# Keys transposed by DMA, a reordered state-space part, and sums copied by two engines in a decoder layer

## The reference

```python
# mixer(x): xn = rmsnorm(x); two Mamba2 passes, forward on channels 0:64, backward in time on 64:128;
#           each: in-projection, causal convolution of width 4, SiLU, state recurrence over 1024 steps,
#           y = (scan + D * xs) * silu(z), y = rmsnorm(y) * w, out-projection; x + concat @ op_w.T + op_b
x = layernorm(x + mixer(x))
q = layernorm(x) @ Wq + bq;  k, v = split(concat([layernorm(ctx), layernorm(x)]) @ Wkv + bkv)   # 8 heads of 128
x = layernorm(x + softmax(q @ k.T / sqrt(128)) @ v @ Wo + bo)
x = layernorm(x + shared_expert(xn) + top2_of_8_experts(xn))      # xn = layernorm(x)
```

## Time and profile before

| | |
|---|---|
| median of 3 runs | 1732.46 us (1732.25 to 1732.76) |
| profiled execution | 1731.69 us, span of its instructions 1729.7 us |
| PE busy | 1673.7 us (97%) |
| DVE busy | 1306.2 us (76%) |
| ACT busy | 1087.5 us (63%) |
| POOL busy | 882.5 us (51%) |
| mean granted TensorE clock | 0.988 of 2.4 GHz |
| HBM read and written | 15.27 MB, 4.23 MB |

### The profile page before, as it was taken

How to read it: one execution, slowest core, us unless ns; L and a number is a source line. 1 busy time by engine, 2 the same in 40 slices (tenths; PEclk the granted TensorE clock), 3 DMA queues, 4 the chain that set the end, 5 groups by cost and what they waited for, 6 DMA issues and landing times.

```text
span 1729.7 us, 32116 instructions
## 1 busy us (share of the span) xinstructions
PE 1673.7 (97%) x9213; PEld 856.4 (50%) x9213; DVE 1306.2 (76%) x2302; ACT 1087.5 (63%) x1333; POOL 882.5 (51%) x724
## 2 busy tenths in 40 slices
PE   6878999999999999999999999999999999999996
PEld 4855444444444444445444444445454544444585
DVE  7968998877777767777777777776767777777667
ACT  4555666666666666666666666666566666667664
POOL 4845994035454545454555545454545454551365
PEclk9989999999999999999999999999999999999998
DMA  5001110000000000000000000000000000000201
GB/s 183 2 1 37 56 55 5 1 1 1 1 0 1 0 0 0 0 0 0 0 0 1 0 0 1 1 0 1 0 0 0 1 0 0 0 1 1 55 25 44
DMA packets 20611, 20.58 MB, mean 12 GB/s; under 512 B 6655, under 2 KB 18179, under 8 KB 20150
## 3 DMA queue, kind: packets, MB, share of 16 engines
q1 hardware_dynamic: 19414, 17.20, 3.2%
q0 software_dynamic: 1120, 2.31, 0.4%
HBM read 15.27 MB, written 4.23 MB: 11 GB/s over the span
## 4 chain that ended last, share of the span: by engine, by line
PE 88%; DVE 4%; ACT 3%; issue 3%; POOL 1%; DMA 1%; SPq 0%; ACTq 0%; POOLq 0%; DVEq 0%
PE PS L1936 87%; ACT p_arena L1095 1%; POOL xg_dram L849 1%; DVE mxs L1790 1%; ACT p_arena L1088 1%; POOL p_arena L858 0%; PE PS L2265 0%; SPq L651 0%; DVE w_arena L1278 0%; DVE w_arena L1452 0%; DMA a_arena<-xg_dram 0%; DMA w_arena<-in_x 0%; ACT z_arena L925 0%; DVE z_arena L1834 0%; ACT p_arena L1079 0%
## 5 line engine op out<-in xcount | busy, mean ns | idle before, releaser
L803 POOL TENSOR_TENSOR p_arena<-p_arena 128x512 f16<-128x512 f32 x364 | 604.3, 1660 | 668.4 <-ACT p_arena L1088 668.4
L1079 ACT ACTIVATE p_arena<-PS 128x1024 f16<-128x1024 f32 (+1 forms) x480 | 484.8, 1010 | 504.8 <-PE PS L1936 504.6
L1497 DVE TENSOR_REDUCE mxs<-PS 128x512 f32 (+1 forms) x900 | 600.5, 671 | 197.2 <-PE PS L1936 195.2
L1936 PE MATMUL PS<-a_arena,z_arena 128*128 128x512 f16 (+1 forms) x2832 | 747.2, 380 | 1.4 <-DVE a_arena L1805 1.4
L1936 PE MATMUL PS<-p_arena,z_arena 128*128 128x512 f16 x2800 | 740.4, 379 | 1.4 <-ACT p_arena L1095 0.3
L1088 ACT ACTIVATE p_arena<-PS 128x1024 f32<-128x1024 f32 (+1 forms) x480 | 481.6, 1003 | 0.0
L1529 DVE TENSOR_TENSOR p_arena<-p_arena 128x512 f16<-128x512 f32 (+1 forms) x480 | 381.5, 795 | 97.9 <-ACT p_arena L1088 91.8
L1936 PEld LDWEIGHTS PS<-a_arena,z_arena 128*128 (+1 forms) x2832 | 274.6, 98 | 326.5 <-issue 2.2
L1936 PEld LDWEIGHTS PS<-p_arena,z_arena 128*128 128x128 f16 (+1 forms) x2800 | 270.5, 98 | 318.0 <-ACT p_arena L1095 8.8
L1936 PE MATMUL PS<-z_arena,a_arena 128*128 (+3 forms) x1024 | 353.9, 361 | 3.1 <-DVE mxs L1790 1.3
L1936 PEld LDWEIGHTS PS<-z_arena,a_arena 128*128 128x128 f16 (+1 forms) x1024 | 98.3, 98 | 123.2 <-DVE mxs L1790 4.5
(11 more groups left out here) (328 smaller groups left out, 1022.4 us busy)
## 6 DMA issues: line engine op xcount, KB each, us to landing
w_arena<-in_L_ffn_gate_up_w SPq DMA_DIRECT2D x8, 512.0 KB, 3.3
p_arena<-in_ctx SPq DMA_DIRECT2D x2, 1600.0 KB, 9.2
w_arena<-in_L_ffn_down_w SPq DMA_DIRECT2D x8, 256.0 KB, 3.7
a_arena<-in_L_xattn_Wkv SPq DMA_DIRECT2D x1, 1024.0 KB, 5.8
a_arena<-xg_dram SPq DMA_DIRECT2D x12, 65.0 KB, 2.0
xg_dram<-VO SPq DMA_DIRECT2D x1, 715.0 KB, 7.6
xg_dram<-VO SPq DMA_DIRECT2D x1, 650.0 KB, 9.0
w_arena<-in_x SPq DMA_DIRECT2D x1, 512.0 KB, 4.3
```

The lines of the kernel that those rows point to most:

```text
L803: g.tensor_tensor(Plo[:, r % 3, QB:2 * QB], P32[:, r % 2, QB:2 * QB], Phi[:, r % 3, QB:2 * QB], ALU.subtract).then_inc(pl_ready, 1)
L1079: s.activation(Phi[:, r % 3, 0:w], ps, ACT.Exp, scale=1 / SSC).then_inc(hi_ready, 1)
L1497: v.tensor_reduce(mxs[:, i, bass.ds(kb, 1)], PS[:, 6 + par, 0:w], AX.X, ALU.max).then_inc(mx_read, 1)
L1936: return t.matmul(o, l, r, start=start, stop=stop)
```

## The change

1. **Keys by DMA.** The 50 context chunks are no longer transposed by PE and copied by ACT. SP issues DMA transfers with transposition from `Zhi` to `ZThi` (28, 14 and 8 chunks, after the casts they need and after the last gated row, since the target memory was in use by then) and from `Zlo` to `ZTlo` (28 and 22 chunks). Only the four left rows stay with PE and ACT (`turned_left`). PE waits for all high keys before the first product of the maxes, for the low ones after the last.
2. **State-space part.** Convolution 0 goes before the second group of dt products; the three products for the decays come after convolution 2 instead of 3, and eight instead of ten convolutions run ahead of the loop. `rows` is split into `decay_rows` and `turned_rows`, which with `gram(0)` go between convolutions 4 and 7, each waiting only for the SiLUs it needs. Aggregates and root of the context's first half move from before the loop into chunk 0; the other side work moves one chunk later.
3. **Early roots.** The sums of squares of chunks 0 to 5 (`SOON`) are brought together in chunk 6 and their root is taken in chunk 7; ACT loads the root's table in chunk 5. Behind the loop 12 of the 16 additions to x are done first, those of chunks 6 and 7 (`LATER`) after a second root, some statistics between. The last multiplication of each Newton step is joined with the scaling after it. The latents' rows are signalled in two halves, and `a_side(0)` starts after the first.
4. **Bias rows** lie in other memory, are loaded before the context and split by POOL before the diagonal matrices.
5. **Order behind the loop**: casts 5, 6 and 7 between the projections, the left keys after the second, the root of the latents between heads 1 and 2. In the maxes the projections of the later heads start one pair later.
6. **Sums.** At step 1 of a block ACT copies bank 4 and DVE bank 5; PE waits for both.

The diff, cut to its core (lines that are only moved or renamed are left out where they repeat the list above):

```diff
@@ -354,6 +353,8 @@
         take = carve(r_arena)
         R0, R00 = take([2, QB])[0:1], take([2, QB])[0:1]
         take = carve(r_arena)
+        brow = take([H * D])
+        take = carve(r_arena)
         xfT = take([T])
...
         CONV = [(0, 0), (0, 1), (0, 2), (1, 0), (1, 1), (1, 2), (0, 3), (1, 3)]
-        AHEAD = 2
+        BESIDE = 4
+        NSOON = 6
+        SOON, LATER = slice(0, NSOON), slice(NSOON, TC)
         DECAY, TURNED_XB, GRAM, STATE, FROM_STATE, INSIDE, GATE = range(7)
         def conv_bank(n):
-            return (1, 2, 3, 4, 5, 6, 7, 1, 7, 6)[n] if n < 8 + AHEAD else 7
+            return (6, 1, 2, 3, 4, 5, 7, 6)[n] if n < 8 else 7
...
-        N_KEYS = len(KV_GROUPS) + 1
-        KEYS_FIRST = 10
-        BEHIND_LOOP = [("out", 0), ("wide", 0), ("keys", 2), ("keys", 3), ("joint", 0), ("wide", 1), ("cast", 6), ("keys", 4), ("root", 0),
-                       ("keys", 5), ("joint", 1), ("cast", 7), ("wide", 2), ("keys", 6), ("keys", 7), ("left", 0), ("joint", 2),
-                       ("latents", 0), ("keys", 8), ("keys", 9)]
...
+        BEHIND_LOOP = [("out", 0), ("cast", 5), ("wide", 0), ("cast", 6), ("joint", 0), ("cast", 7), ("wide", 1), ("left", 0), ("joint", 1),
+                       ("root", 0), ("wide", 2), ("joint", 2), ("latents", 0)]
+        LATE0 = 2
...
+            def turned_keys(s_parts, first, parts, src, dst, done):
+                sp.wait_ge(s_parts, first + parts.stop)
+                c0, w = CTX0 + HI_PARTS[parts.start][0], sum(HI_PARTS[i][1] for i in parts)
+                sp.dma_start(dst[:, c0 * P:(c0 + w) * P].rearrange("p (c n) -> p c n", n=P), src[:, c0:c0 + w, :],
+                             transpose=True).then_inc(done, 16)
+            sp.wait_ge(yg_done, TC)
+            for parts in HI_TURNS:
+                turned_keys(z_hi, 0, parts, Zhi, ZThi, zt_hi)
             sp.wait_ge(z_lo, 1)
             sp.dma_start(Zhi[32:32 + LEFT, 0, :], Zlo[0:LEFT, 0, :]).then_inc(left_st, 16)
             sp.dma_start(Zhi[64:64 + LEFT, 0, :], Zhi[0:LEFT, 0, :]).then_inc(left_st, 16)
+            for parts in LOW_TURNS:
+                turned_keys(z_lo, 1, parts, Zlo, ZTlo, zt_lo)
             sp.wait_ge(zlT_v, 2)
             sp.wait_ge(z_lo, N_HI + 1)
...
-            pool.wait_ge(ld_mw, N_MW)
-            for q in range(2):
-                last = g.tensor_scalar(diagD[:, q], I32[:], V["D_" + "fb"[q]], None, ALU.mult)
-            last.then_inc(diag_ready, 1)
-            pool.wait_ge(ld_b, 48)
+            pool.wait_ge(ld_nd, N_ND)
             g.tensor_scalar(brow[0:3, :], brow[0:3, :], BS, None, ALU.mult).then_inc(brow_ready, 1)
             pool.wait_ge(brow_ready, 1)
             g.tensor_copy(b16[0:3, :], brow[0:3, :]).then_inc(brow_ready, 1)
             pool.wait_ge(brow_ready, 2)
             g.tensor_tensor(b16[32:35, :], brow[0:3, :], b16[0:3, :], ALU.subtract).then_inc(brow_ready, 1)
             pool.wait_ge(brow_ready, 3)
+            pool.wait_ge(ld_mw, N_MW)
...
-                if c == 0:
-                    for n in range(8, 8 + AHEAD):
-                        silu_conv(n)
-                if c < 3:
-                    silu_conv(8 + AHEAD + 2 * c)
+                if c < BESIDE:
+                    silu_conv(8 + 2 * c)
+                if c == TC - 1:
+                    root(2)
+                if 2 <= c < NSOON - 1:
+                    high_ctx(c - 2)
+                elif c == NSOON - 1:
+                    s.activation(rt[:, 5, 0:1], iota8[:, 0:1], ACT.Sqrt)
+                elif c == NSOON:
+                    high_ctx(c - 3)
                 if c:
-                if c >= 2:
-                    silu_conv(9 + AHEAD + 2 * c)
+                if c < BESIDE:
+                    silu_conv(9 + 2 * c)
                 act.wait_ge(yg_done, c + 1)
                 for q in range(2):
                     if c or q:
                         act.wait_ge(sq_done, 2 * c + q)
...
+            for n in range(6):
                 silu_conv(n)
             state_rows(0)
+            for n in range(6, 8):
+                silu_conv(n)
             for c in range(TC):
...
-            for k in range(2):
-                turned_keys(k, ZThi, zt_hi)
+            high_ctx(4)
+            gate_out(TC - 1)
+            root(3)
...
-                    turned_keys(k, ZThi, zt_hi)
                 elif kind == "root":
-                    root(3)
+                    root(4)
                 elif kind == "left":
                     act.wait_ge(z_scaled, CC + 1)
                     s.copy(Zhi[0:LEFT, 0, :], ctxl[:]).then_inc(z_hi, 1)
+                    turned_left(ZThi, 1, 2)
...
-                s.copy(U_sb, PS[:, 4:6, :]).then_inc(u_evac, 1)
+                s.copy(U_sb[:, 0], PS[:, 4, :]).then_inc(u_evac, 1)
...
                 dve.wait_ge(sq_out, k)
-                settle(v.reciprocal(rs[:, 3, 0:w], rs[:, 1, 0:w]))
+                settle(v.tensor_tensor(at(1), at(3), at(3), ALU.mult))
+                settle(v.tensor_tensor(at(1), at(1), at(0), ALU.mult))
+                settle(v.tensor_scalar(at(1), at(1), -0.5, 1.5, ALU.mult, ALU.add))
...
@@ -1388,6 +1379,8 @@
                 dve.wait_ge(yi_ps, c + 1)
                 dve.wait_ge(t1_done, c + 1)
+                if c == 0:
+                    dve.wait_ge(silu_done, 8)
                 if c >= 2:
                     dve.wait_ge(gt_ps, c - 1)
...
+                if c == TC - 1:
+                    dve.wait_ge(z_scaled, CC // 2)
                     inputs(c + 1)
...
                     settle(v.bn_stats(st6[0:LEFT, CC, :], ctxl[:]))
-                elif c == 2:
+                elif c == 3:
                     ctx_aggr(CC // 2, CC)
                     settle(v.bn_aggr(mv[0:LEFT, CC, :], st6[0:LEFT, CC, :]))
                     for piece in range(5):
                         last = v.tensor_copy(VO[:, h, :, D:D + 1], I32[:, 0:1].unsqueeze(1).to_broadcast([P, 2, 1]))
                     last.then_inc(t_ready, 1)
+                    dve.wait_ge(ss_ps, 1)
+                    dve.wait_ge(sq_done, 2 * NSOON)
+                    chunk_root(2, SOON, PS[:, 7, SOON])
+            def mixed_in(q, part):
+                for c in range(TC)[part]:
+                    t, at = place(q, c), q * TC + c
+                                                  op0=ALU.mult, op1=ALU.add)
+                return last
...
+            dve.wait_ge(out_evac, NSOON)
+            mixed_in(0, SOON)
+            dve.wait_ge(ss_ps, 2)
+            dve.wait_ge(sq_done, 2 * TC)
+            chunk_root(3, LATER, PS[:, 0, 0:TC - NSOON])
+            settle(mixed_in(1, SOON))
+            row_stats(range(TC - NSOON, NSOON))
+            chunk_scale(3, LATER)
             dve.wait_ge(out_evac, TC)
-            dve.wait_ge(z_scaled, CC + 1)
+            mixed_in(0, LATER)
+            settle(mixed_in(1, LATER))
...
-            dve.wait_ge(sq_done, 2 * TC)
-            v.tensor_copy(ssy[:, 1, :], PS[:, 0, 0:TC]).then_inc(yo_used, 1)
-            dve.wait_ge(yo_used, 1)
-            inv_root(2, 2 * TC, ssy[:].rearrange("p q c -> p (q c)"), 1.0 / D)
-            for q in range(2):
-                for c in range(TC):
-                    at = q * TC + c
-                    if c == 0 and q:
-                        settle(last)
-                    last = v.scalar_tensor_tensor(out=x_sb[:, c, :], in0=yo[:, q, c, :], scalar=rs[:, 3, at:at + 1], in1=x_sb[:, c, :],
-                                                  op0=ALU.mult, op1=ALU.add)
...
+                return v.tensor_scalar(dst, src, mv[:, t, 0:1], rs[:, 3, at + t:at + t + 1], ALU.subtract, ALU.mult)
...
+            v.tensor_scalar(rs[:, 0, TC:2 * TC], mv[:, 0:TC, 1], 1.0 + EPS, EPS * EPS, ALU.mult, ALU.add).then_inc(sq_in, 1)
+            for half in range(2):
+                for c in range(HT * half, HT * half + HT):
+                    last = norm_row(zl[:, c, 1:D], x_sb[:, c, 1:D], c, TC)
+                last.then_inc(zl_ready, 1)
...
+                    if st == 1 and not first:
+                        dve.wait_ge(pv_done, NS * j)
+                        v.tensor_copy(U_sb[:, 1], PS[:, 5, :]).then_inc(u_evac, 1)
...
+            pe.wait_ge(w_sb, 2)
+            for n, (q, b) in enumerate(X_ORDER):
+                pe.wait_ge(xT_lo, n + 1)
+                if n == 1:
+                    convolve(0)
...
+            convolve(1)
...
             convolve(2)
-            convolve(3)
...
+                if c < BESIDE:
+                    convolve(9 + 2 * c)
+                if c == NSOON:
+                    pe.wait_ge(sq_done, 2 * NSOON)
+                    mm(PS[:, 7, SOON], J32[:], ssy[:, 1, SOON]).then_inc(ss_ps, 1)
+            convolve(3)
+            convolve(4)
             pe.wait_ge(dt_a, 4)
-            pe.wait_ge(silu_done, 8)
+            decay_rows(0)
+            convolve(5)
+            pe.wait_ge(op_sb, 3)
+            convolve(6)
+            pe.wait_ge(silu_done, 5)
+            turned_rows(0)
+            pe.wait_ge(silu_done, 6)
```

(23 more changed lines are left out.)

232 lines of the change are left out of this document (85 added, 147 removed).

## The result

The changed kernel took 1723.92 us (median of 5 executions, 1721.67 to 1724.7) beside 1732.76 for the kernel before: the ratio is 0.9945, with a 95% interval of 0.993 to 0.9959. It is 8.8 us faster where 14.4 were forecast; the time lies in the forecast range (1709 to 1731), but the likeliest case (1713 to 1722) missed it by 2 us. The profiled execution is the shortest of the five (1721.67, span 1719.7; before 1731.69 and 1729.7), so its rows explain 10.0 us.

The account below looks back on a forecast made before the run. PE bounds the middle blocks, a chain of waits the stretch behind the chunk loop. Gains of 7.3 (to the first product), 3.5 (maxes) and 3.6 (sums) make 14.4: 1731.7 - 14.4 + 0.8 = 1718 us, range 1709 to 1731.

Parts of the forecast that it names:

- likeliest case: Whole kernel: the forecast of 1713 to 1722 us, given a chance of 0.5.
- First mixing: Ahead of the chunk loop: first mixing at 37.25 us instead of 44.60, 7.35 us earlier.
- Chunk loop: State-space chunk loop: 53.3 us against 47.28, giving back 6.0 of the 7.35; last gated row at 94.4.
- Behind the loop: Last gated row to first product for the maxes: 18.65 us instead of 25.21; first product 7.3 us earlier in absolute time.
- PE at half clock behind the loop: Rival: without the keys PE has gaps behind the chunk loop and its clock falls; maxes up to 4 us later; chance 0.2.
- Maxes: Loop of 30 first maxes: 3.5 us gained, with nearly no keys for PE to turn and DVE setting the later pace.
- Copy of the sums: Step 1 of each block: splitting the copy between ACT and DVE removes PE's stall, 15 x 0.24 = 3.6 us gained.
- Transposes: Keys by DMA: hidden, high ones within 18.65 us of the last gated row, low ones during the maxes.
- Early roots: Behind the chunk loop: that they do nothing, since ACT's order sets the second root, was in the forecast in part.

Follow-up runs that it names:

- sums_act: The changed kernel with ACT again copying both banks of the sums in all 15 places, DVE none; 1725.69 us, ratio 0.995.
- keys_alone: The kernel before with only the keys' transposition by DMA (part 1 of the change) added; 1732.82 us, ratio 0.9988.
- fill_maxes: The changed kernel plus 24 products that nobody reads on PE in pairs 19 to 24 of the first maxes; 1720.57 us, ratio 0.9919.
- fill_all: The changed kernel plus products nobody reads in the last chunk and behind it, in the maxes, and ahead of block 0; 1716.75 us, ratio 0.989.

## Why the prediction was off, step by step

- **First mixing**: 37.25 forecast, 37.56 measured. Right, with its steps: exponential at 30.15 (30.4), six SiLUs from 31.82 (32.1).
- **Chunk loop**: 53.3 us forecast from first to last mixing, 51.11 measured. Chunk 0 took 9.91 (9.85). The largest miss is chunk 4, 5.42 us where I left it at 7.42: before, the clock was at 1.2 GHz from 71.5 to 75.5, around its start (0.76 and 0.91 in the two stretches there), DVE waited 1.7 us for PE in it, and I took that for work. That it was the clock is read from these rows; no run isolates it. Chunk 3 was dearer (10.69 for 9.34), chunks 1 and 2 cheaper (6.92 and 7.33 for 7.83 each). Last gated row 92.01, not 94.4.
- **Behind the loop**: 18.65 forecast. This is the step that failed: "with them it is ready for the second root at 9.6", measured 8.5, but the root at 13.4, not 12.0, because head 0 ran at 1.2 GHz. At full clock the same kernel took 17.69, so the chain (ACT in order, DVE waits about 2.2; measured 2.57) was right, though DVE was ready 1.1 us sooner than forecast and the root came at 10.7. The clock then added 2.7 us, and 20.39 is 1.7 over the forecast. It is the rival *PE at half clock behind the loop* (up to 4 us, 1722 to 1726), which had 0.2: its mechanism is in the profiled execution, and the median, 1723.92, lies in its range. The first product came at 112.40 where 113.05 was forecast. That is luck: 2.4 us too long up to the last gated row and 1.7 too short behind it.
- **Maxes**: 3.5 forecast, 0.69 measured, 3.5 at full clock and with fillers (38.02 us). This is the dearest step that failed, 2.8 us: I had "the clock staying low as now" at the start, and didn't ask what taking 13 groups of low keys out of PE in this loop does to it later. The clock was full at the start and low from 142.5 to 149.5. So that full clock gives just the 3.5 forecast is partly luck. The rival had the place behind the loop only.
- **Copy of the sums**: 15 x 0.24 = 3.6 forecast; 3.3 gained (13 x 0.25), and 0.92 lost in the fifteenth place. I had looked at what DVE has queued in a middle block, not at the last block, where `front_in_block` stands ahead of the copy.
- **Transposes**: hidden, as forecast; 0.28 to 0.39 us a chunk, where the nearest row said 0.18 and the bound was 0.37 for all 50; they were all there 12.6 us after the last gated row. The transfer of 65 KB as a price one after the other (1.0) turned out near the truth for single chunks (1.29), though what it prices is their issue and not the transfer.
- **Early roots**: 0.5 us at the first product with ACT late by the clock; the forecast has them idled away in part.
- **The end**: 0.77 us of the 1.69 lost behind the fifteenth copy stays open. From that copy to the end it was 173.38 us before, 174.99 to 175.07 in the changed kernel, but 173.92 in sums_act and 175.28 in keys_alone, whose copies are those of before; part of it differs from execution to execution.

Added up against the 14.4 of the forecast: 0.65 more up to the first product, 2.8 less in the maxes, 0.3 lost to the first copied sums, 0.3 less at the sums, and 1.7 lost behind the fifteenth copy, which leaves the 10.0 of the profiled execution.

At full clock, 17.69 and 38.02 would take 5.5 us off that execution: about 1716, an estimate, and near the two shortest executions (1715.70, 1715.93), of which there is no trace. So at full clock the kernel is some 2 us faster than the forecast, and by the medians of its two sets 3 to 6 us slower. That it was idle PE that lost the clock in the maxes rests on the ten profiles compared under fill_maxes; behind the loop it rests on the clocks of fill_all, and is less sure. That the same kernel loses it in one execution and not in another is shown, but why isn't.

## What to carry to other kernels

When work is taken off TensorE, ask where its row of the profile gets thin, and reckon with products at 1.2 GHz behind that place, or move other work there (with a whole head more to do the maxes took 37.5 us instead of 39.5 to 41.0). When an instruction is queued once per block on an in-order engine, look at what stands before it in the first and in the last block, not only in the middle. And before an early result is built, check which engine issues the next step: here DVE's early roots moved the first product by 0.5 us, and ACT's early root didn't move it while three heads stood ahead. When two variants are compared, compare their clock too: keys_alone looked like 0.95 us behind the loop, and at equal clock it is nearer 3.5.

## What the hardware showed that I had not expected

- A transposing DMA holds the issuing queue: 1.23 us for 32 KB alone, 4.33 us for 28 such chunks, which also land at 0.28 us each. Fifty single ones took 64.4 us, in which SP issued nothing else.
- The granted clock in the same kernel differs between executions (0.986 to 0.995 of 2.4 GHz on average), and with it the time by 9 us; with the gaps filled it was 0.995 to 0.998 and the times within 2 us.
- The price of 1.2 GHz in a chain of several engines depends on the place. Behind the loop 7 us of it cost 2.7 us and 13.5 us 5.3, in the maxes 7 us cost 2.8 and 3.5 us 1.5: about 0.4 us for each. With two heads ahead 7 us more of it cost 1.5 behind the loop (17.79 for 16.26). Ahead of the chunk loop 7 us cost 0.15 (first mixing at 37.71 for 37.56) and 10.5 us 1.9 (39.31 for 37.40).
